# A routed expert stage cut into 56 units of 512 rows and 24 of 256, with rows asked for six units ahead

## What is computed

```python
shared = gelu(x @ W1s + b1s) @ W2s + b2s
rw = softmax(x @ Wr)                    # 8 experts
topw, topi = top_k(rw, 2); topw = topw / sum(topw)
h = gelu(einsum('bsd,edf->bsef', x, W1p) + b1p)      # 128 -> 512
priv = einsum('bsef,efd->bsed', h, W2p) + b2p        # 512 -> 128
out = x + shared + sum of the two chosen experts' priv, by topw
```

## Time and profile before

| | |
|---|---|
| median of 3 | 1564.83 us |
| the profiled execution, its own time | 1566.65 us |
| its span, first to last instruction | 1564.8 us |
| busy over the span | PE 79%, DVE 70%, ACT 63%, POOL 56% |
| mean granted TensorE clock (1.0 is 2.4 GHz) | 0.939 |
| routed stage | 943 to 1486 us |

### The profile page before, as it was taken

One profiled execution on the slowest core, in us unless ns is written; L12 is line 12 of the kernel. 1 busy time (PEld: TensorE's weight loads), 2 busy tenths in 40 slices (PEclk: granted clock), 3 DMA queues, 4 the chain that ended last, 5 costly groups with the idle time before them and its releaser, 6 DMA issues. The chain is left out here.

```text
span 1564.8 us, 33624 instructions
## 1 busy us (share of the span) xinstructions
PE 1238.3 (79%) x9505; PEld 706.7 (45%) x9506; DVE 1101.2 (70%) x2467; ACT 984.6 (63%) x1713; POOL 876.4 (56%) x922
## 2 busy tenths in 40 slices
PE   2999999999999999837899977888888888878300
PEld 1566666666666666623344433333443333334100
DVE  3688898888899888845677764555565555555288
ACT  1677777777777777625677766676776767667200
POOL 3246666666666666536756652556565656555500
PEclk9999999999999999968899998999999999999755
DMA  2012222122222211122354322333233333333099
GB/s 59 28 55 64 68 67 65 62 65 63 65 67 67 66 62 47 42 68 75 109 147 126 115 62 51 72 65 79 67 74 67 75 69 77 67 67 80 10 333 312
DMA packets 225698, 128.33 MB, mean 82 GB/s; under 512 B 128175, under 2 KB 203998, under 8 KB 225644
## 3 DMA queue, kind: packets, MB, share of 16 engines
q1 hardware_dynamic: 191596, 85.44, 21.6%
q0 software_dynamic: 17408, 33.87, 6.4%
q10 hardware_dynamic: 16640, 8.39, 1.8%
HBM read 47.37 MB, written 55.09 MB: 65 GB/s over the span
## 5 line engine op out<-in xcount | busy, mean ns | idle before, releaser
L935 DVE SCALAR_TENSOR_TENSOR h<-hid,h 128x512 f16<-128x512 f32 x416 | 286.1, 693 | 265.6 <-ACT h L915 223.3
L1224 POOL DMA_INDIRECT pairs_dram<-x_rows x288 | 294.1, 1021 | 104.1 <-issue 104.0
L915 ACT ACTIVATE h<-hid 128x512 f16<-128x512 f32 x416 | 261.9, 630 | 57.8 <-remote 10.6
L887 PE MATMUL Y<-h,w 128*128 128x512 f16 x1248 | 292.0, 384 | 7.1 <-DVE h L935 4.4
L876 PE MATMUL Z<-x_rows,w 128*128 128x512 f16 x864 | 209.8, 395 | 93.0 <-issue 76.3
L926 ACT ACTIVATE hid<-Z,biases 128x512 f32<-128x512 f32 x416 | 279.8, 673 | 0.0
L887 PEld LDWEIGHTS Y<-h,w 128*128 (+1 forms) x1248 | 122.5, 99 | 163.9 <-issue 22.3
L419 DVE TENSOR_REDUCE smax<-S 128x8 f32<-128x1024 f32 x128 | 155.8, 1217 | 47.4 <-PE S L642 47.4
L1029 POOL DMA_INDIRECT slots_dram<-x_rows,pair_slot x140 | 143.4, 1024 | 70.5 <-issue 40.6
L876 PEld LDWEIGHTS Z<-x_rows,w 128*128 x864 | 81.8, 101 | 201.0 <-issue 121.5
L422 DVE TENSOR_TENSOR probs<-S,smax 128x1024 f32<-128x1024 f32 x128 | 156.8, 1225 | 16.1 <-DVE smax L419 3.4
(11 more groups left out here) (165 smaller groups left out, 2092.5 us busy)
## 6 DMA issues: line engine op xcount, KB each, us to landing
y_pairs<-pairs_dram SPq DMA_DIRECT2D x32, 512.0 KB, 6.0
x_res<-in_x_dram SPq DMA_DIRECT2D x32, 256.0 KB, 3.2
adj<-in_adj_dram SPq DMA_DIRECT2D x32, 256.0 KB, 3.0
x_rows<-x SPq DMA_DIRECT2D x32, 256.0 KB
xT_dram<-xT SPq DMA_DIRECT2D x32, 256.0 KB
xTu<-xT_dram SPq DMA_DIRECT2D x32, 256.0 KB
out_dram<-x_res ACTq DMA_DIRECT2D x16, 512.0 KB, 10.1
pairs_dram<-x_rows POOLq DMA_INDIRECT x288
```

The source lines that it names most:

```text
L887: mm = pe.matmul(self.Yt[:, b], self.w2[:, m, :, c][:, e, :], self.h16[:, b, k, c], start=c == 0 and n == 0, stop=c == FC - 1 and n == 2)
L915: act.activation(self.h16[:, b, 0, c], self.hid[:, c], ACT.Copy, scale=HS).then_inc(self.hi_done, 1)
L935: dve.scalar_tensor_tensor(out=self.h16[:, b, 1, c], in0=self.hid[:, c], scalar=HS, in1=self.h16[:, b, 0, c], op0=ALU.mult, op1=ALU.subtra ...
L1224: pool.indirect_dma_start(pairs_dram, bass.IndirectOffsetOnAxis(ap=pair_of[n][:, j:j + 1], axis=0), y_sb[n % NIN][:, j], None, bounds_chec ...
```

## The change

The routed stage gets two sizes of unit. WHOLE = 64 - 8 = 56 units have 512 rows and take only full blocks of 512 of an expert, in the experts' order, until 56 are given out. What is left of each expert, 4096 rows in all, goes into 24 units of HALF = 256 rows (16, and up to one part filled for each expert). So 80 units pass the pipeline, with 56 x 512 + 24 x 256 = 34816 rows in place of 72 x 512 = 36864.

All parts of a unit take the width w: matmuls, activations and copies have 256 columns in a half unit, `back` 2 transposes and `send` 2 indirect DMAs in place of 4. The number of matmuls, activations and DVE instructions of a unit is otherwise the same. Around the seam each part uses the width of its own unit.

xT has 8 buffers in place of 4 and y has 2 in place of 4; the load of unit u waits for the copy of unit u-6 in place of u-4, and `keep_y` waits for the sends of u-2 in place of u-4.

```diff
-NU = TOP * NT * P // UT + E
+WHOLE = TOP * NT * P // UT - E
+HALF = UT // 2
+NU = WHOLE + (TOP * NT * P - WHOLE * UT) // HALF + E
...
-    def hidden(self, pe, u, e, b):
+    def hidden(self, pe, u, e, b, w=UT):
...
-                mm = pe.matmul(self.Z[:, c], self.w1[:, k, :, c * P:(c + 1) * P][:, e, :], self.xT[:, b, m],
+                mm = pe.matmul(self.Z[:, c, 0:w], self.w1[:, k, :, c * P:(c + 1) * P][:, e, :], self.xT[:, b, m, 0:w],
...
-    NIN = 4
-    NID = 8
+    NY = 2
+    NIN = 8
+    LEAD = 6
...
-        for u in range(NID):
-            unit(u, u)
-        with eng.Fori(1, U // NID - 1) as r:
-            for n in range(NID):
-                unit(NID * r + n, n)
-        for n in range(NID):
-            unit(U - NID + n, n)
+        for u in range(NIN):
+            unit(u, u, UT, UT, UT)
+        with eng.Fori(1, WHOLE // NIN) as r:
+            for n in range(NIN):
+                unit(NIN * r + n, n, UT, UT, UT)
+        for n in range(NIN):
+            unit(WHOLE + n, n, HALF, HALF if n >= 1 else UT, HALF if n >= 2 else UT)
+        with eng.Fori(WHOLE // NIN + 1, NU // NIN) as r:
+            for n in range(NIN):
+                unit(NIN * r + n, n, HALF, HALF, HALF)
...
-            if not early(u, NIN):
-                sp.wait_ge(f.back_read, u + 1 - NIN)
+            if not early(u, LEAD):
+                sp.wait_ge(f.back_read, u + 1 - LEAD)
...
-            if not early(u, NIN):
-                dve.wait_ge(sent[n], turns(u, n) * GT)
-            dve.tensor_copy(y_sb[n], f.B7[:, :].rearrange("p (j c) -> p j c", j=GT)).then_inc(f.back_read, 1)
+            if not early(u, NY):
+                dve.wait_ge(sent[n], sends_before(u, n, w))
+            dve.tensor_copy(y_sb[n][:, 0:w // P], f.B7[:, 0:w].rearrange("p (j c) -> p j c", c=P)).then_inc(f.back_read, 1)
```

More of the change, by code:

```diff
@@ L963, in shared_phase @@
     stride = sb("stride", [P, E])
+    whole = sb("whole", [P, E + 1])
+    upto = sb("upto", [P, E])
+    half_stride = sb("half_stride", [P, E])
     expert_f = sb("expert_f", [1, NU])
@@ L1107, in units_of_experts @@
             then(dve.tensor_tensor(count[:], rt.tot[:], rt.base[:], ALU.subtract))
-            then(dve.tensor_scalar(need[:], count[:], float(UT - 1), None, ALU.add))
-            then(dve.tensor_copy(need_i[:], need[:]))
+            then(dve.tensor_copy(need_i[:], count[:]))
             then(dve.tensor_scalar(need_i[:], need_i[:], UT.bit_length() - 1, None, ALU.logical_shift_right))
             then(dve.tensor_copy(need[:], need_i[:]))
-            then(dve.memset(first[:, 0:1], 0.0))
+            then(dve.tensor_copy(upto[:, 0:1], need[:, 0:1]))
@@ L1113, in units_of_experts @@
             for e in range(1, E):
-                then(dve.tensor_tensor(first[:, e:e + 1], first[:, e - 1:e], need[:, e - 1:e], ALU.add))
-            then(dve.tensor_tensor(last[:], first[:], need[:], ALU.add))
-            then(dve.tensor_scalar(stride[:], need[:], -float(UT), float(REGION), ALU.mult, ALU.add))
+                then(dve.tensor_tensor(upto[:, e:e + 1], upto[:, e - 1:e], need[:, e:e + 1], ALU.add))
+            then(dve.tensor_scalar(upto[:], upto[:], float(WHOLE), None, ALU.min))
@@ new lines, in units_of_experts @@
+            then(dve.memset(whole[:, E:E + 1], 0.0))
+            then(dve.tensor_copy(whole[:, 0:1], upto[:, 0:1]))
+            then(dve.tensor_tensor(whole[:, 1:E], upto[:, 1:E], upto[:, 0:E - 1], ALU.subtract))
+            then(dve.tensor_scalar(stride[:], whole[:, 0:E], -float(UT), float(REGION), ALU.mult, ALU.add))
+            then(dve.scalar_tensor_tensor(out=need[:], in0=whole[:, 0:E], scalar=-float(UT), in1=count[:],
+                                          op0=ALU.mult, op1=ALU.add))
@@ new lines, in units_of_experts @@
+            then(dve.tensor_scalar(need[:], need[:], float(HALF - 1), None, ALU.add))
+            then(dve.tensor_copy(need_i[:], need[:]))
+            then(dve.tensor_scalar(need_i[:], need_i[:], HALF.bit_length() - 1, None, ALU.logical_shift_right))
+            then(dve.tensor_copy(need[:], need_i[:]))
+            then(dve.tensor_scalar(last[:, 0:1], need[:, 0:1], float(WHOLE), None, ALU.add))
+            for e in range(1, E):
+                then(dve.tensor_tensor(last[:, e:e + 1], last[:, e - 1:e], need[:, e:e + 1], ALU.add))
@@ new lines, in units_of_experts @@
+            then(dve.tensor_tensor(half_stride[:], whole[:, 1:E + 1], whole[:, 0:E], ALU.subtract))
+            then(dve.tensor_scalar(half_stride[:], half_stride[:], float(UT), float(REGION), ALU.mult, ALU.add))
+            then(dve.scalar_tensor_tensor(out=half_stride[:], in0=need[:], scalar=-float(HALF), in1=half_stride[:],
+                                          op0=ALU.mult, op1=ALU.add))
+            then(dve.tensor_scalar(first[:, 0:1], whole[:, 0:1], float(UT), -float(WHOLE * HALF), ALU.mult, ALU.add))
@@ L1127, in table_of_units @@
             then(dve.tensor_copy(rt.unit_expert[:], expert_f[:]))
-            then(dve.scalar_tensor_tensor(out=start_f[:], in0=unit_ids[:], scalar=float(UT), in1=start_f[:],
-                                          op0=ALU.mult, op1=ALU.add))
+            then(dve.tensor_scalar(start_f[:, WHOLE:NU], start_f[:, WHOLE:NU], first[0:1, 0:1], None, ALU.add))
+            for units, rows in ((slice(0, WHOLE), UT), (slice(WHOLE, NU), HALF)):
+                then(dve.scalar_tensor_tensor(out=start_f[:, units], in0=unit_ids[:, units], scalar=float(rows),
+                                              in1=start_f[:, units], op0=ALU.mult, op1=ALU.add))
             then(dve.tensor_scalar(start_f[:], start_f[:], float(BLANK), None, ALU.min))
@@ L1218, in _, with send @@
     def _(pool):
-        def send(u, n):
+        def send(u, n, w, w1, w2):
             pool.wait_ge(f.back_read, u + 1)
-            pool.wait_ge(numbers_in[n], (u - n) * (16 // NID) + 16)
+            pool.wait_ge(numbers_in[n], turns(u, n, NIN) + 16)
             f.take_wait(pool, u)
-            for j in range(GT):
+            for j in range(w // P):
                 pool.indirect_dma_start(
```

105 lines of the change are left out of this document (56 added, 49 removed).

## The result

The changed kernel takes 1537.84 us, the median of 4 executions (1535.83 to 1540.68), beside 1564.89 for the kernel before on the same chip: a ratio of 0.983, 95% interval 0.9809 to 0.985. The profiled execution took 1537.59 us, with a span of 1535.8.

What follows compares the result with a forecast made beforehand. A ring of copy, load and matmuls was taken to bind the routed stage. Whole units 358.4, half units 101.2, end 13.9 and tables 3 made 476.5 us for 529.0, so 1513 us, 3.3% faster; range 1468 to 1550.

Steps and rivals of the forecast that it cites:

- The ring: Routed stage: copy, load and matmuls make 14.2 us over two units, 7.1 a unit; with six units' lead it binds nowhere.
- What is late next: Whole units, once the lead is six: PE 5.62 and POOL 5.7 us, plus late counts; 6.4 taken, 358.4 us for 56.
- late counts: Shared stage: PE's counts reached ACT only when PE had run dry, after 4.63 us idle; expected in the routed stage too.
- the floor 5.7: Whole units: the shortest period that the engines' own work allows, 5.7 us, with 6.73 as the other end.
- Half units: Units of 256 rows: 4.4 us each, set by PE's instruction stream, 101.2 us for 23 starts; ends 3.6 and 5.6.
- Two y buffers: DVE's copies into y, waiting for the sends of u-2: nothing taken; 8 us in all if landing takes 6.0.
- Tables: Shared stage: 23 more small DVE instructions for the units' table, 4.7 us, part hidden; 3 taken, ends 0 and 5.
- The end: From the last unit's start to POOL's end: 13.9 us against 23.7; the last 8.2 us and the last stage stay.
- (a): Rival: PE's counts come in time, whole units come down to 5.75 us, 36 us less, 1477; chance 0.26.
- (b): Rival: the array runs at 1.2 GHz in the half units, 5.6 us a unit, 28 us more, 1541; chance 0.11.
- (c): Rival: POOL or the sends' landing holds whole units at about 7.1 us, 39 us more, 1552; chance 0.07.
- (d): Rival: slower than before, counts late in nearly each second unit, whole periods from 7.3 us, 1614; chance 0.06.

Runs made afterwards that it cites:

- group 3: Four follow-up kernels on chip 11: the changed kernel unedited and three edits of it run again; the kernel before took 1571.44 us there.
- group 2: Four follow-up kernels, edits of the changed kernel, which itself was not run; the kernel before took 1534.24 us there.
- e7_reuse: Changed kernel with PE keeping the expert's number from hidden to output in seven units of eight; 1436.2 us, ratio 0.9354.
- e2_sizes: Changed kernel with rows asked for four units ahead instead of six; 1582.2 us, ratio 1.0104.
- e3_ny4: Changed kernel with four y buffers instead of two, SP also waiting for the sends of u-8; 1558.2 us, ratio 0.9918.
- e1_lead: Kernel before with eight xT buffers and rows asked for six units ahead, units and y buffers unchanged; 1569.7 us, ratio 0.9997.
- e8_same: Changed kernel without an edit, run again beside others on chip 11; 1557.4 us, ratio 0.99.
- e9_queue_again: Changed kernel with a whole unit's output held until half of the next unit's Z is counted; 1555.4 us, ratio 0.9896.
- e10_reuse_again: Changed kernel with PE keeping the expert's number from hidden to output in seven units of eight, on chip 11; 1552.7 us, ratio 0.9872.
- e4_gap: Changed kernel with PE's transposes in each whole unit's cycle waiting for the last Gelu, leaving PE idle; 1539.0 us, ratio 0.9812.
- group 1: Four follow-up kernels testing the change's parts alone, y buffers and idle time; the kernel before took 1570.28 us there.

## Why the prediction came out as it did

The profiled execution was expected at 1514 and took 1537.6: the sum was some 23 us short. The gain in the median is 27 us of the 52 forecast. Of the prediction's own signs, whole units 6.1 to 6.8 apart and half units 4.2 to 4.6, both are missed by a little (6.84 and 4.62). The time lies inside the range of 1468 to 1550, and there is luck in that: in group 3 the same kernel took 1557.4, and in group 2 e7_reuse, whose edit is worth next to nothing, took 1436.2. The range knew nothing of the condition on which the gaps depend. By the prediction's steps:

- **The ring**: right. Added up to 7.1 a unit, it gives 7.14 when it is put back (e2_sizes). With six units of lead PE's waits ahead of Z fall from 76.3 to 11.0 us, while SP goes on waiting.
- **What is late next**: right in kind. The late counts of the earlier trace rows did come along, as 16 "remote" waits of ACT. Their price is the term that was mis-sized. 56 whole units took 1331.7 - 948.9 = 382.8 us for the 358.4 expected, 24.4 more, about all that is missing. The step that failed is the choice of 6.4 between the floor 5.7 and the shared stage's 6.73. I had discounted the stage's mean for DVE's splitting of weights there, but nothing shows that this work has a part in it: the routed stage, without it, got 6.84, and where the gaps are absent the shared stage with it runs at 5.89. The mean of the shared stage was the better estimate: 56 x 6.73 = 376.9, and some 1532.6 for the profiled execution.
- **Half units**: 106.3 us for 101.2. Without the two gaps at units 56 and 58 (9.2 and 10.0 for some 4.1) it would be 95.3, or 4.14 each; steady ones are at 4.02. So two errors partly cancel: 4.4 a unit was too long, and the two gaps weren't in the sum. The reason given for the 4.4, PE's instruction stream, isn't borne out either: with one of the two reads of the expert's number gone the distance stays 4.02 (e7_reuse). By the groups of after, ten half units from 1385 to 1425, ACT has little room there:

```profile
L928 ACT ACTIVATE hid<-Z,biases 128x256 f32<-128x256 f32 x39 | 18.0, 461 | 0.0
...
L917 ACT ACTIVATE h<-hid 128x256 f16<-128x256 f32 x38 | 15.8, 416 | 3.4 <-DVE h L937 0.4 <-ACT hid L928 0.2
```

  4 x 0.461 + 4 x 0.416 + 0.2 = 3.7 of 4.02 us. I had bounded ACT at 3.6. The wait for Z, 0.36 us ahead of most units, brings it to about 4. Whether ACT or the sequencer sets the 4.02 wasn't tried.
- **Two y buffers**: next to nothing, as taken. DVE waits ahead of L1302 three times, 5.2 us in all; e3_ny4 shows no gain from four.
- **Tables**: 3 expected, 1 to 3 seen. The routed stage starts at 948.9 for 948.6, but in this execution the shared stage starts 2.5 us earlier (716.3 for 718.8). From the first unit of the one to the first of the other it is 232.6 us for 229.8, and 231.5 in e1_lead (720.6 to 952.1), which has the tables of the kernel before. The recorded 4.7 us for 23 instructions of 0.2 should read 4.6.
- **The end**: 13.9 expected, 1451.9 - 1438.0 = 13.9 measured. The wait for the last sends' landing is shorter by 2.3 us than taken (1457.77 - 1451.9 = 5.9 for 8.2). The last batch is two sends in place of four, which may be why; it wasn't tried.
- **Rivals.** (a), counts in time, is what group 2 shows: e7_reuse, which in group 3 differs from the changed kernel by 4.7 us only, is 0.9354 there. For the change itself that is an inference: it wasn't run in group 2. (b) is out: half units are at 4.02 and the clock at 1.00 but for some 14 us behind two gaps. The Trainium skill's "TensorE: Matmul & The Clock Gate", section "Why this matters for your kernels", would have thin matmuls swing the clock unless they are grouped or padded; here it stays up. In e2_sizes, with the same widths and waits of PE of up to 3.8 us ahead of them, it is 0.90 in the mean. (c) is out: POOL waits for DVE's copy, not the reverse, and at 5.60 a unit POOL still keeps up. (d) wants 7.3 a unit; with gaps in two units of five e8_same came to 7.16. It was nearer than its chance of 0.06 says: the gain over the kernel before was 1.0% in that group.

**What stays open** is the cause of the gaps. The runs show what it isn't: the y buffers, a long queue of PE (e9_queue_again shortens it), the second read of the expert's number (e10_reuse_again; the first was never taken away), DVE's splitting of weights, the load on the DMA engines (91 GB/s at a share of 0.44 without gaps, 75 at 0.36 with them), a lower granted clock (1.00 in the gap from 1212 to 1217.2), or a gapless PE by itself. What brings them belongs to the chip or to its condition at the time; the two can't be told apart here. Each execution has a granted clock from the profiler's records, so none is known to have run unrecorded, and a part of the recording in the gaps isn't ruled out. Where the gaps are present, PE's busy share over the whole units comes out at 86 to 88% in every kernel that isn't held by the ring, whether the idle time is spread by a wait (e4_gap, 88%) or falls in gaps (86 to 87%). That is a regularity of eight profiles, not a mechanism. The busy time rests on modelled ends of matmuls. And the gain has two halves that don't add: the lead alone 0.9997 and the sizes alone 1.0104 in group 1, both together 0.983 in the first comparison and 0.99 in group 3.

## What to carry to other kernels

When a change closes the gaps of an engine, look for a stage of the same kernel in which it already runs without gaps, and take that stage's mean, with its stalls, for the new one; don't discount it by a guess at what else differs. It is an estimate, and no more: the shared and the whole units came 6.76 and 6.84 apart in the first comparison, 6.76 and 7.16 in group 3, 5.89 and 5.60 in e7_reuse. A ring that spans several units is found by adding up one turn of it and dividing by the units that it spans, and it can be checked by putting the old distance back. Before a cure is believed, compare a stage that it doesn't touch: here four "cures" ran at 0.935 to 0.954 while the gaps were absent from the shared stage too, and three of them, run again where the gaps were, gained nothing that can be told from the changed kernel.

## What the runs showed of the hardware

- TensorE's counts can be late for the engines that wait for them, by 2.1 to 6.2 us of ACT's idle time, 16 times in the routed stage; in the rows shown the matmuls ahead are gapless. In the one gap looked at closely PE's sequencer is slow too, an instruction of 18 ns taking 719. The first gap comes some 30 us into gapless work (at unit 5 in all five kernels with gaps and no idle time built in), the next ones mostly every two or three units.
- One and the same program differs by this between groups of runs: the kernel before 1534.24 or 1571.44 us, e7_reuse and e10_reuse_again (the same kernel) 1436.2 or 1552.7. The gain of the change is 1.0 to 1.7% with the gaps, and about 6.5% by e7_reuse without them.
- Half units, 24 matmuls of 256 columns and two transposes in some 4 us, kept the granted clock at 1.00 over their last 58 us, with PE busy 78%. In e2_sizes, where PE stands up to 3.8 us ahead of the hidden matmuls, the mean was 0.90.
